# One kernel of eight stages: transformer scores made a second time in turned form, and expert weights loaded ahead

## The reference

```python
# sixth block: 8 experts, each row goes to 2 of them; H = 8 heads of 32
def _expert(x, Wqkv, bqkv, Wo, bo, g1, be1, W1, bf1, W2, bf2, g2, be2):
    q, k, v = heads of (x @ Wqkv.T + bqkv)
    attn = softmax((q / sqrt(32)) @ k.T)            # over all 1354 keys
    ctx = (attn @ v) @ Wo.T + bo
    x = layernorm(x + ctx, g1, be1)
    h = gelu(gelu(x @ W1.T + bf1) @ W2.T + bf2)     # hidden width 1024
    return layernorm(x + h, g2, be2)
# fourth block: out = shared SwiGLU(x) + sum over 2 of 8 experts of weight * expert_out[e] @ swiglu(x @ in)
# eighth block: sum over 2 of 8 experts of weight * layernorm(relu(x @ W1[e] + b1[e]) @ W2[e] + b2[e], gamma, beta)
```

## Time and profile before

| | us |
|---|---|
| median of 3 runs (lowest, highest) | 3118.02 (3117.1, 3120.5) |
| the profiled execution's own time | 3119.24 |
| its span | 3117.5 |
| PE busy in the span | 2457.1 (79%) |
| DVE busy | 1568.1 (50%) |
| ACT busy | 1143.3 (37%) |
| POOL busy | 522.6 (17%) |
| first scores of the attention loop | at 1663.07 |
| last maximum | at 2733.1 |

### The profile page before, as it was taken

One profiled execution on the slowest core, in us unless ns is written; L12 is line 12 of the kernel. 1 busy time (PEld: TensorE's weight loads), 2 busy tenths in 40 slices (PEclk: granted clock), 3 DMA queues, 4 the chain that ended last, 5 costly groups with the idle time before them and its releaser, 6 DMA issues. The chain is left out here.

```text
span 3117.5 us, 52757 instructions
## 1 busy us (share of the span) xinstructions
PE 2457.1 (79%) x18627; PEld 2058.2 (66%) x18627; DVE 1568.1 (50%) x3095; ACT 1143.3 (37%) x2211; POOL 522.6 (17%) x818
## 2 busy tenths in 40 slices
PE   6979589769977748875785999999888998964256
PEld 4858589769956634764784777777777777744244
DVE  3636512232236741143444776777776777742355
ACT  2323222112213211122223656665656566624422
POOL 0000022122202100510001111122221122110043
PEclk9989699779978969987897999999999999976678
DMA  4000023124341101730565231334145452112066
GB/s 125 1 7 1 18 89 91 52 93 147 91 99 63 36 28 46 265 105 22 223 260 166 75 106 37 83 97 124 52 134 152 112 142 66 25 45 51 1 225 209
DMA packets 147050, 293.50 MB, mean 94 GB/s; under 512 B 37155, under 2 KB 74057, under 8 KB 143717
## 3 DMA queue, kind: packets, MB, share of 16 engines
q1 hardware_dynamic: 127988, 237.43, 24.8%
q0 software_dynamic: 18800, 52.69, 6.1%
HBM read 488.56 MB, written 65.74 MB: 178 GB/s over the span
## 5 line engine op out<-in xcount | busy, mean ns | idle before, releaser
L2226 PE MATMUL tx_ring<-g_ident,tx_p 128*128 128x128 f32 x2552 | 395.9, 283 | 75.3 <-DVE tx_p_t L2470 35.8
L2226 PEld LDWEIGHTS tx_ring<-g_ident,tx_p 128*128 128x128 f32 x2552 | 287.1, 142 | 178.9 <-DVE tx_p_t L2470 58.6
L2470 DVE COPY tx_p_t<-tx_ring 128x512 f32<-128x512 f32 x464 | 305.7, 684 | 129.6 <-PE tx_ring L2226 126.4
L2463 DVE TENSOR_REDUCE tx_neg_max<-tx_scores 128x1 f32<-128x1354 f32 x232 | 362.0, 1561 | 17.6 <-PE tx_scores L2214 17.6
L2360 ACT ACTIVATE tx_p<-tx_scores,tx_neg_max 128x1354 f32<-128x1354 f32 x232 | 322.8, 1392 | 87.2 <-DVE tx_neg_max L2463 84.7
L2367 ACT ACTIVATE tx_p_t<-tx_ring 128x384 f32<-128x384 f32 x232 | 113.7, 490 | 291.1 <-PE tx_ring L2226 287.3
L2214 PE MATMUL tx_scores<-tx_keys,tx_queries 96*128 96x512 f32 (+1 forms) x696 | 203.2, 401 | 14.9 <-DMA tx_queries<-tx_q_hi 11.2
L2266 PE MATMUL tx_ring<-tx_p_t,tx_values 128*32 128x128 f32 x5104 | 170.7, 295 | 13.2 <-ACT tx_p_t L2367 12.7
L2266 PEld LDWEIGHTS tx_ring<-tx_p_t,tx_values 128*32 128x32 f32 x5104 | 152.9, 119 | 26.7 <-ACT tx_p_t L2367 23.9
L2214 PEld LDWEIGHTS tx_scores<-tx_keys,tx_queries 96*128 96x128 f32 x696 | 115.9, 193 | 25.5 <-issue 14.9
L192 PE MATMUL ln_turned<-g_ident,g_xn 128*128 128x128 f32 x176 | 39.4, 408 | 117.5 <-DVE g_xn L179 117.5
(11 more groups left out here) (957 smaller groups left out, 5278.3 us busy)
## 6 DMA issues: line engine op xcount, KB each, us to landing
tx_keys<-expert_keys SPq DMA_DIRECT2D x696, 169.5 KB
lv1e_w<-in_L_ffn_W SPq DMA_DIRECT2D x232, 256.0 KB
tx_w<-in_L_ffn_W SPq DMA_DIRECT2D x58, 1024.0 KB
lv0e_w<-in_L_ffn_W SPq DMA_DIRECT2D x200, 256.0 KB
tx_values<-expert_values SPq DMA_DIRECT2D x58, 704.0 KB
tx_rows<-in_L_ffn_rows SPq DMA_DIRECT2D x29, 640.0 KB, 3.7
sro_we<-_L_ffn_expert_out_weight SPq DMA_DIRECT2D x29, 512.0 KB, 5.6
nee_w<-in_L_ffn_w SPq DMA_DIRECT2D x58, 256.0 KB, 4.3
```

The costliest lines, as they stand in the source:

```text
L2226: last = nc.tensor.transpose(ring[u % 2][:, (t - t0) * P:(t - t0 + 1) * P], p[n % 2][:, t * P:(t + 1) * P], g.ident[:])
L2463: nc.vector.tensor_reduce(neg_max[:, n % 4:n % 4 + 1], sc[n % 2][:, 0:N], AX_X, ALU.max, negate=True)\
L2470: nc.vector.tensor_copy(p_t[:, n % TURNED, t0:t0 + nt, :], ring[u % 2][:, 0:nt * P].rearrange("p (t q) -> p t q", q=P))\
```

## The change

Three edits.

In the attention loop, `p`, its transposes and their copies go. The scores of rows (`scores`) serve for the maximum only, in one buffer of three banks. GpSimd splits the negated maximum in two parts (`split_maxima`), TensorE turns them with a one into three rows (`turn_maxima`), and ScalarE writes these as rows 96 to 98 of `queries`. Rows 96 to 98 of `keys` hold one (and a far negative number in the padding), so that `turned_scores`, 99 rows deep, gives score minus maximum with keys on the partitions, in a ring of five banks; ScalarE's exp goes from there to `p_t`, which has six buffers. The sums over keys of heads 4 to 7 are products with ones in the lanes of `mix` (`sums`); for heads 0 to 3 VectorE sums over the eleven blocks (`sum_keys`) and one product with ones sums over partitions. `context` takes the reciprocal of 128 columns from PSUM. GpSimd's work for a tile is spread over the heads.

In the fourth block all weights are loaded in the `early` of its norm (`RoutedWeights`), the eight experts' `we` among them, and TensorE reads the tile's owner into a register. In the eighth likewise (`NormedWeights`); TensorE, ScalarE and VectorE read the owner, and ScalarE copies the tile's `w1` to a fixed place (`bring`).

```diff
-TURNED = 5
-PE_EXTRAS = {0: ("inverse1", "values1"), 1: ("output", "turn_rows"), 2: ("queries",), 3: ("turn_middle",), 4: ("inverse0", "values0"),
+TURNED = 6
+RING = 5
+CONSTS = 1
+ROWS_ON_PE = (4, 5, 6, 7)
+QM = QR + 3
+FAR = -1e30
+PE_EXTRAS = {0: ("values1", "sums1"), 1: ("turn_rows", "output"), 2: ("queries",), 3: ("turn_middle",), 4: ("values0", "sums0"),
...
-        keys, values = s.sb("keys", [QR, HEADS, NT], F32R), s.sb("values", [P, 2, NB, P])
+        keys, values = s.sb("keys", [QM, HEADS, NP], F32R), s.sb("values", [P, 2, NB, P])
...
-        sc = [s.ps(f"scores{i}", [P, CH * BANK]) for i in range(2)]
-        ring = [s.ps(f"ring{i}", [P, BANK]) for i in range(2)]
+        sc = s.ps("scores", [P, CH * BANK])
+        ring = [s.ps(f"ring{i}", [P, BANK]) for i in range(RING)]
...
-                        sync.wait_ge(s_full, HEADS * i + hd + 1)
+                        sync.wait_ge(full, at["heads", i, (hd, CH - 1)] + 1)
...
-                if n >= 2:
-                    pe.wait_ge(exp_done, n - 1)
+                if n:
+                    pe.wait_ge(max_done, n)
                 for k0, w in KCH:
-                    last = nc.tensor.matmul(sc[n % 2][:, k0:k0 + w], queries[:, i % 2, hd, :], keys[:, hd, k0:k0 + w],
+                    last = nc.tensor.matmul(sc[:, k0:k0 + w], queries[0:QR, i % 2, hd, :], keys[0:QR, hd, k0:k0 + w],
                                             start=True, stop=True)
                 last.then_inc(s_full, 1)
 
-            def turn(i, hd, c):
+            def turn_maxima(n):
+                u = at["maxima", n, 0]
+                free(pe, u)
+                pe.wait_ge(max_split, n + 1)
+                nc.tensor.matmul(ring[u % RING][QR:QM, 0:P], max_parts[:, n % 4, :].bitcast(F32), g.ident[:], start=True, stop=True,
+                                 tile_position=(0, QR)).then_inc(full, 1)
+
+            def turned_scores(i, hd, c):
                 u, n = at["heads", i, (hd, c)], HEADS * i + hd
                 free(pe, u)
                 if c == 0:
-                    pe.wait_ge(exp_done, n + 1)
-                    pe.wait_ge(const_made, 3)
+                    written(pe, at["maxima", n, 0])
+                    pe.wait_ge(const_made, CONSTS)
                 t0, nt = TG[c]
                 for t in range(t0, t0 + nt):
-                    last = nc.tensor.transpose(ring[u % 2][:, (t - t0) * P:(t - t0 + 1) * P], p[n % 2][:, t * P:(t + 1) * P],
-                                               g.ident[:])
+                    last = nc.tensor.matmul(ring[u % RING][:, (t - t0) * P:(t - t0 + 1) * P], keys[:, hd, t * P:(t + 1) * P],
+                                            queries[:, i % 2, hd, :], start=True, stop=True)
...
+            def sums(i, half):
+                u = at[f"sums{half}", i, 0]
+                free(pe, u)
+                for t in range(NB):
+                    for lane in range(HEADS // 2):
+                        hd = 4 * half + lane
+                        if hd in ROWS_ON_PE:
+                            last = nc.tensor.matmul(ring[u % RING][HD * lane:HD * (lane + 1), 0:P], ones[:],
+                                                    p_t[:, (HEADS * i + hd) % TURNED, t, :], start=(t == 0), stop=(t == NB - 1),
+                                                    tile_position=(0, HD * lane))
+                for lane in range(HEADS // 2):
+                    hd = 4 * half + lane
+                    if hd not in ROWS_ON_PE:
+                        pe.wait_ge(summed, summed_by(i, hd))
+                        last = nc.tensor.matmul(ring[u % RING][HD * lane:HD * (lane + 1), 0:P], ones[:],
+                                                over_keys[:, half, lane, :], start=True, stop=True, tile_position=(0, HD * lane))
                 last.then_inc(full, 1)
...
+                        for c in range(CH):
+                            turned_scores(i, hd, c)
+                        if n + 1 < heads:
+                            turn_maxima(n + 1)
+                        if n + AHEAD < heads:
+                            scores(n + AHEAD)
                     if hd == 0 and i:
-                        turn_inverse(i - 1, 1)
                         mix(i - 1, 1)
+                        sums(i - 1, 1)
                     if hd == 1:
+                        if i + 1 < tiles:
+                            turn_rows(i + 1)
                         if i:
...
+            def exponent(i, hd, c):
+                u, n = at["heads", i, (hd, c)], HEADS * i + hd
                 act.wait_ge(full, u + 1)
-                nc.scalar.activation(p_t[:, n % TURNED, t0:t0 + nt, :], ring[u % 2][:, 0:nt * P].rearrange("p (t q) -> p t q", q=P),
-                                     ACT.Copy).then_inc(drained["act"], 1)
...
+                t0, nt = TG[c]
+                nc.scalar.activation(p_t[:, n % TURNED, t0:t0 + nt, :],
+                                     ring[u % RING][:, 0:nt * P].rearrange("p (t q) -> p t q", q=P), ACT.Exp)\
+                    .then_inc(drained["act"], 1)
+
+            def keep_maxima(n):
+                u = at["maxima", n, 0]
+                act.wait_ge(full, u + 1)
+                nc.scalar.activation(queries[QR:QM, n // HEADS % 2, n % HEADS, :], ring[u % RING][QR:QM, 0:P], ACT.Copy)\
+                    .then_inc(drained["act"], 1)
...
+            def sum_keys(n):
+                i, hd = n // HEADS, n % HEADS
+                if hd in ROWS_ON_PE:
+                    return
+                written(dve, at["heads", i, (hd, CH - 1)])
+                if i:
+                    dve.wait_ge(full, at[f"sums{hd // 4}", i - 1, 0] + 1)
+                nc.vector.tensor_reduce(over_keys[:, hd // 4, hd % 4, :], p_t[:, n % TURNED, :, :].rearrange("p t q -> p q t"),
+                                        AX_X, ALU.add).then_inc(summed, 1)
...
+                link(nc.vector.reciprocal(inv_t[:, half, :], ring[below % RING][:, 0:P]))
+                nc.vector.tensor_tensor(ctx_t[:, half, :], ring[u % RING][:, 0:P], inv_t[:, half, :], ALU.mult)\
+                    .then_inc(drained["dve"], 2)
...
+                    if 0 < n <= heads:
+                        sum_keys(n - 1)
+                    if n + AHEAD < heads:
+                        row_max(n + AHEAD)
...
+            own(nc.gpsimd.memset(minus_half[:], -0.5))
+            own(nc.gpsimd.memset(ones[:], 1.0))
+            own(nc.gpsimd.memset(max_parts[:, :, 0:1].bitcast(F32), 1.0))
+            own(nc.gpsimd.memset(keys[0:QR, :, NT:NP].bitcast(F32), 0.0))
+            own(nc.gpsimd.memset(keys[QR:QM, :, :].bitcast(F32), 1.0))
+            own(nc.gpsimd.memset(keys[QR:QR + 1, :, 0:N].bitcast(F32), 0.0))
+            nc.gpsimd.memset(keys[QR:QR + 1, :, N:NP].bitcast(F32), FAR).then_inc(const_made, 1)
+            pool.wait_ge(const_made, CONSTS)
+
+            def split_maxima(n):
+                pool.wait_ge(max_done, n + 1)
+                if n >= 4:
+                    pool.wait_ge(full, at["maxima", n - 4, 0] + 1)
+                own(nc.gpsimd.tensor_copy(max_parts[:, n % 4, 1:2], neg_max[:, n % 4:n % 4 + 1]))
+                nc.gpsimd.tensor_tensor(max_parts[:, n % 4, 2:3], neg_max[:, n % 4:n % 4 + 1], max_parts[:, n % 4, 1:2],
+                                        ALU.subtract).then_inc(max_split, 1)
...
+    def load(self, sync):
+        a = self.a
...
+        for i, name in enumerate(("L1_ffn_shared_in_w", "L1_ffn_expert_in_w")):
+            sync.dma_start(self.w_in[i][:], a[name].rearrange("(k p) o -> p k o", p=P)).then_inc(self.w_in_loaded[i], 16)
+        sync.dma_start(self.ws[:], a["L1_ffn_shared_out_w"].rearrange("(k p) o -> p k o", p=P)).then_inc(self.ws_loaded, 16)
+        for e in range(self.experts):
+            sync.dma_start(self.we[:, e, :, :].rearrange("p k o -> p (k o)"), a["L1_ffn_expert_out_weight"][e])\
+                .then_inc(self.we_loaded, 16)
...
-            def load(i):
-                k = i % ROUTED_SETS
-                new = dict(cond=expert(i) != expert(i - ROUTED_SETS)) if i >= ROUTED_SETS else {}
-                sync.dma_start(we[:, k, :, :].rearrange("p k o -> p (k o)"),
-                               expert_dram[bass.ds(expert(i), 1)].rearrange("o p n -> p (o n)"), **new).then_inc(we_loaded[k], 16)
-
...
             back.load_table(sync)
-            for i in range(ROUTED_SETS, tiles):
-                sync.wait_ge(done, i - ROUTED_SETS + 1)
-                load(i)
             back.load(sync, sent, all_sent)
...
+                if i == 0:
+                    pe.wait_ge(we_loaded, 16 * plan.experts)
...
+                    last = nc.tensor.matmul(row[i % 2][:, 0:D], hg_t[:, i % 2, f, :], we[:, of(i), f, :].rearrange("p o n -> p (o n)"),
...
+def owners(eng, plan):
+
+    held = {}
+
+    def of(i):
+        if i not in held:
+            held[i] = eng.value_load(plan.owner[0:1, i:i + 1], min_val=0, max_val=plan.experts - 1)
+        return bass.ds(held[i], 1)
+    return of
...
+class NormedWeights:
...
```

(22 more changed lines are left out.)

375 lines of the change are left out of this document (160 added, 215 removed).

## The result

The changed kernel takes 3348.03 us (median of four runs, 3344.72 to 3359.57) against 3118.48 (four runs, 3117.10 to 3120.50) for the kernel before: ratio 1.0742, interval 1.0715 to 1.0769. That is 230 us slower. The forecast was 3146, range 3088 to 3258: the direction was right, and the loss was eight times what I summed. The changed kernel's four totals lie 15 us apart, so a difference of that size between two single runs tells nothing. Where the attention loop is the old one it repeats better: 1068.5 to 1069.9 us in four profiles (before, e1_bc, e2_b, e12_bc4).

A forecast was written before the change was run, and what follows sets the result against it. TensorE was taken to pace the attention loop. Loop +47, tail +3, start +18 and the fourth and eighth blocks -42 gave +26 on the profiled 3119.24: 3145, stated as 3146 us, range 3088 to 3258.

The forecast's parts named there:

- 34.8 us of work: Attention loop, TensorE: about 30.2 us of products a tile plus 4.6 of new work.
- 4.3 of waits: Attention loop, TensorE: new waits a tile for maxima, VectorE's run and the values' banks, 4.3 us.
- 1.6 us for a sum over 1408: Attention loop, VectorE: each strided sum over keys priced at 1.04 ns an element, 1.6 us.
- rival (3): Attention loop: VectorE's strided sums take 3.2 us, 4.9 more a tile on the path, total 3283; chance 0.07.
- rival (2): Attention loop: narrow one-pass products cost as plain ones, 0.229 us, total about 3255 to 3300; chance 0.16.
- 1.8 waited: Attention loop, first four heads: VectorE's about 12 us against TensorE's 10.2, so TensorE waits 1.8 us a tile.
- 39.2 a tile: Attention loop: forecast period of a tile, work plus waits, 39.1 to 39.4 us against 37.55.
- The base of the period: Attention loop before the change: one tile read as 37.55 us, from which the period's +1.7 was taken, times 28.
- The fills: Attention stage's start: seven fills ahead of GpSimd's first fetch take 20 us instead of 0.3, giving +18 us.
- B: Fourth (routed) block: weights loaded ahead and a shorter tile loop, about -22 us; loop bounded at 70 us.
- Rival (1): Attention loop: five banks and early scores remove nearly all waits, total 3088; chance 0.24.
- B and C, -42: Routed fourth and normalised eighth blocks: early weights gain 17 us, loops 9 and 16; -42, range -20 to -52.

The follow-up runs named there:

- e1_bc: Kernel before with only the early loads and register reads of the fourth and eighth blocks, old attention stage: 3089.92 us, ratio 0.9908.
- e2_b: Kernel before with the fourth block's edit alone: 3091.74 us, ratio 0.9912.
- e12_bc4: e1_bc with the eighth block's 33 early transfers issued as 5: 3084.6 us, ratio 0.9885.
- e14_nosums: e8_sum1 with TensorE's products with ones also over one block instead of eleven, so no sum is whole: 3137.8 us, loop 1102.9.
- e8_sum1: Changed kernel with VectorE's sums over one block of keys instead of eleven, so not the softmax's: 3248.76 us, loop 1186.1.
- e3_contig: Changed kernel with VectorE's sums reading 1408 elements side by side, so other keys are summed together: 3266.31 us, loop 1229.8.
- e9_early: Changed kernel with VectorE's sum of head 0 moved ahead of the wait for the previous tile's context: 3309.47 us, loop 1273.2.
- e13_sum1_wide: e8_sum1 with query columns streamed twice in nine of eleven turned products: 3181.4 us, loop 1142.7.
- e15_wide_contig: e3_contig with query columns streamed twice in nine of eleven turned products: 3223.81 us, loop 1181.3.
- e4_pe8: Changed kernel with the sums of all eight heads as products with ones on TensorE, none on VectorE: 3316.76 us, loop 1276.8.
- e16_wide_pe8: Changed kernel with all sums on TensorE, query columns streamed twice, and fills off the first fetch's path: 3228.96 us, ratio 1.0361.
- e5_wide: Changed kernel with query columns streamed twice in nine of a head's eleven turned products: 3367.34 us, loop 1304.1.
- e17: Changed kernel with head 0's sum ahead of the context, query columns streamed twice, and mended fills: 3298.62 us, loop 1274.6.
- e6: Changed kernel with six unread plain products ahead of the turning of the maxima of heads 2, 3 and 4: 3362.38 us, loop 1302.2.
- e10_layout: Changed kernel with probabilities stored so sums read side by side; ScalarE writes and TensorE reads with a stride: 3469.95 us, loop 1428.5.

## Why the prediction missed

In the prediction's own terms a tile had 34.8 us of work and 4.3 of waits. Measured, it takes 45.3 (1307.2 over 231 steps, eight to a tile), 6.2 more. About 4.1 of them are the lower clock (the 117 us above), for which the prediction had no term, and about 2.1 are waits: 6.4 in place of 4.3. Both are estimates, with the work left at 34.8.

What causes them is shown by the loop from the bottom up, each step a difference of two kernels that were run (the three in the middle in one run each, on three chips):

| Step | loop, us | adds |
|---|---|---|
| before | 1068.5 | |
| turned scores, maxima as rows, sums over one block (e14_nosums) | 1102.9 | +34 |
| sums of heads 4 to 7 with ones (e8_sum1) | 1186.1 | +83 |
| VectorE's sums, read side by side (e3_contig) | 1229.8 | +44 |
| the stride of these sums (after) | 1307.2 | +77 |

**Term "1.6 us for a sum over 1408": mis-sized, 2.60.** Its stride alone cost 77 us (shown by e3_contig). The row I priced it by, a maximum, reads side by side. I did see the doubt and put 3.2 as rival (3), 0.07, which would have given 3283. It is the one rival whose mechanism was partly there; rival (2) had the nearer number, up to 3300, by a mechanism that the traces refute.

**Term "1.8 waited": mis-sized.** I summed VectorE's work in the first four heads and compared it with TensorE's. I didn't ask when VectorE can begin. It stands before the context for 4.5 us in the mean, because the sums with ones come last, and only then starts its run, 17.5 us in the tile shown. There TensorE waits 2.02 and 1.66 us for the maxima, 3.7 in place of 1.8. e9_early shows that the order is worth 34 us of the loop.

**A missing term: the clock.** I costed every product at full clock, with the clock row 0.97 in the earlier trace rows before me. The time at 1.2 GHz went from 57 to 300 us. Shown: wide products bring the clock back where waits are short, and then cut the loop by 43 (e8 to e13), 49 (e3 to e15) and 73 us (e4 to e16), but by nothing where VectorE paces (e5, e17). Shown too: in the changed kernel most falls follow long waits, 38 of 46, so the mis-sized waits and the missing clock hang together. So the parts don't add: as long as the sums are slow the clock is hidden behind them, and once they are fast the clock is next. Not shown is how the changed kernel's own 300 us divide between the two: doubled columns took away 69 (e5), filled waits 180 (e6). The forecast's own 39.2 a tile holds nowhere with all of its sums: with sums of 1.6 us and the clock nearly back it is 40.9 (e15_wide_contig). Only e13_sum1_wide comes near, 39.6 in the mean, and its four sums are all but gone, so that this is luck.

**The base of the period.** The tile that I read, 37.55, was slower than the mean: 1068.5 over 231 steps, eight to a tile, is 37.0. At 28 tiles that hid 15 us.

**Right.** Turned products 0.112 apart for 0.115, so rival (2), 0.229, is refuted: a turned product costs what the transpose did, 0.109. The Trainium skill ("TensorE: Matmul & The Clock Gate", section "Terms") gives the transpose mode a lead of four times for FP32; for this one-pass type the runs show none. The fills, 18 for 17.5. The reciprocal, 1.16 for 0.96, near enough. B: the loop 70 for 67.7, and -24 in all for about -22. Rival (1), no waits left, is refuted: idle time rose.

**B and C, -42, measured -27: C was mis-sized.** Its share of the forecast was about 20, measured are 3. For its loop I took GpSimd's 2.59 as the pace and said that the register reads had slack: 70 us for 28 steps, 80.6 measured. The rows show 2.9 a tile, with TensorE waiting for its own issue and ScalarE bringing each tile's weights. That these two set the pace is read from the order of the rows; no kernel without them was run. And the 33 issues on SyncE, which I costed at nothing, hold up the next stage by some 5 us: shown by e12_bc4.

## What to carry to other kernels

Price a reduction by its step between elements, and before turning a layout to please one engine, count the engines that will then stride. After a sum of work per engine, go through the slowest engine's queue and ask when it can start, since an idle stretch in front of a full one is as dear as work. When a change fills TensorE with many small products or makes it wait more often, read the granted clock of each stretch as a term of the sum; and look for the engine that paces before paying to win the clock back.

## What the runs showed of the hardware

- A one-pass product of 128 columns starts 0.112 us after the last. Eleven of them, nine doubled to 256 columns, take 1.28 us from the first to the last start instead of 1.17, so the second 128 columns cost about 0.012 each. Streaming the same columns twice was cheaper than the clock that the narrow ones lost: 1.2 GHz for 35 us instead of 226 (e4_pe8, e16_wide_pe8).
- The granted clock fell behind waits of TensorE. Counted as above, waits of 0.8 to 1.4 us were followed by a fall in 48 of 59 cases with narrow one-pass products (e4_pe8) and in none of 32 with doubled ones (e16_wide_pe8); waits over 1.4 us in 38 of 51 (after) and in 37 of 56 with doubled ones (e5_wide).
- A sum over 1408 fp32 elements: 1612 ns read side by side, 2600 with 512 bytes between them. An exp of 512 columns that writes with 44 bytes between elements: 1106 ns instead of 596. Value products that read their 128 columns so: 88 in 4.81 us instead of 2.34 (e10_layout).
- A reciprocal of 128 columns, read from PSUM, takes 957 ns, where 4 take 170 and 11 take 226: 6.3 ns for each further element, a little less than the 8 from the two small ones.
- A fill of few partitions costs by its length, 0.84 ns an element on GpSimd (9.48 us for 11264) and on VectorE (7.10 us for 8448).
- SyncE needed 0.51 us for each issue of 33 transfers (16.7 us), and the next stage's first product came 0.4 us after the last. Issued as 5, they held SyncE for 10.2 us, 3.40 of them for the biases and 5.20 for the broadcast rows (e12_bc4), and the next stage's first product came 4.9 us earlier after the statistics than in e1_bc.
